# Expert pieces of eight blocks with stationary weights fetched from DRAM per block, on one Trainium2 core

## The chip, the core and the metric

The kernel runs on one core of a Trainium2 chip. The metric is device time in microseconds (us), from start to end of one execution. Within the core TensorE (PE) multiplies matrices, VectorE (DVE), ScalarE (ACT) and GpSimd (POOL) do elementwise work, and SyncE (SP) issues nearly all transfers (DMAs) from one queue, in the order of its program.

## The reference, cut to what matters

Two transformer layers work on x of shape (32, 256, 128). Each has attention with 16 heads of 8 features and then a feed-forward part of 16 experts, of which every token takes two. For the change only the experts matter:

```python
# layer 0 (weights per expert e: gate_up 128x128, down 64x128, with biases)
gate, up = minimum(gate, 7), clip(up, -7, 7)
act = (up + 1) * gate * sigmoid(1.702 * gate)
out = sum over the two chosen e of score_e * (act @ down_e + down_bias_e)
# layer 1 (no biases), plus a shared expert that the change leaves alone
act = silu(x @ Wg_e) * (x @ Wu_e)
out = sum over the two chosen e of w_e * (act @ Wd_e)
```

## The kernel before

**Units and steps.** A unit is one batch entry of one layer: 64 units, 16 heads each. The program of every engine is one loop over `step`; unit u computes the scores of head j at step 16u + j. In every step PE computes two products of scores, of one unit for the maxima (`ps_s`, line 1224) and of the unit before for the exponentials (`ps_st`, line 1230); DVE takes the maximum (line 1639), ACT the exponential (line 871). All engines go through the steps in pairs, here called rounds: a unit has eight. In a round PE issues the scores of both steps first and then `jobs(step)` and `jobs(step + 1)`: projections, transposes, probabilities times values (line 1093), and the experts' pieces. PE takes its instructions in order, so what one job waits for holds up all later ones, the scores too.

**Experts.** Units are taken in nine groups (`SIZES`, 8 units in the first six; groups 0 to 3 are layer 0). The tokens of a group are sorted by expert into blocks of 128 rows in DRAM (`slot_dram`, written by POOL, line 672), 48 blocks for a group of 8 units; a row of integers, `column`, says which expert a block belongs to. Blocks are worked on in pieces of `QB` = 4 (class `Quad`), 100 in all. A piece is loaded (SP, line 535), transposed on PE (line 1044), multiplied by gate and up weights that lie in SBUF for all 16 experts (lines 1061 and 1062), put through tanh and products (ACT, DVE, POOL), transposed back (line 1074), multiplied by the down weights (line 1081), taken by ACT (line 854) and stored (SP, line 545). Between, ACT also copies the two transposes (lines 828 and 847). PE loads the four experts' numbers into registers (line 1051), which are the column offsets into the weights. The outputs stand with tokens in rows.

**What sets the order.** The table `QUAD` gives the step at which each piece is transposed, `STAGE` the distance from it of each later stage; a piece's stages thus fall in fixed rounds. SP's order is the same for its queue. Per unit it issues, at fixed steps: six transfers of the projections to DRAM (`part_rows`, lines 502 and 505, at step 15 of the 16), four of 192 KB that bring them back as stacks (`stack_rows`, line 517, at step 4), the maxima out (`max_store`, line 482, at 7 and 15) and back (`max_rows`, line 492, at 10 and 2), and `mod_in` (line 582, at 12). Two of these wait for other engines at a place that matters below:

```python
def stack_rows(u):                       # SP, step 16u - 12
    ...
    if u.has(3):
        sp.wait_ge(st_mm, u.count(16, -32))
def max_rows(u, half):
    sp.wait_ge(mx_stored[half], u.count(16, 16))
```

The first holds SP at its step 4 until PE has issued the scores of its step 9, because the stacks have three buffers. The second waits until the maxima have landed in DRAM.

Of the kernel before, what the change touches and what calls it, by code (L numbers as in the profile page):

```python
# [41 lines left out]
QB = 4  # L42
# [9 lines left out]
LANES = 3  # L52
# [31 lines left out]
class Quad:  # L84

    def __init__(self, no):
# [11 lines left out]
        self.before_bank = first - 2 + min(self.lane, 1) if start else no - LANES if self.tail else no - 2  # L98
        self.blk = self.bank = self.lane if self.tail else self.par
# [20 lines left out]
for g in range(NG):  # L120
# [18 lines left out]
STAGE = {"blocks": (0, 0), "gate_up": (3, 3), "clip": (3, 3), "tanh": (5, 3), "act": (6, 3), "product": (7, 7), "act_t": (10, 6),  # L139
         "down": (15, 9), "store": (16, 10), "load": (-12, -5)}  # L140


def quad_at(step, stage):

    for quick, after in enumerate(STAGE[stage]):
        q = Quad(QUAD[step - after]) if step - after in QUAD else None
        if q and q.quick == quick:
            return q
# [18 lines left out]
def build(nc, io, out):  # L167
    with ExitStack() as ctx:
# [29 lines left out]
        wgu = [sb(f"wgu{l}", [P, E * 2 * F]) for l in range(2)]  # L198
        wd = [sb(f"wd{l}", [P, E * D]) for l in range(2)]
# [16 lines left out]
        b_stack = sb("b_stack", [P, 2 * E * F], BF16)  # L216
# [53 lines left out]

        g_sb = sb("g_sb", [P, QB, F])
        u_sb = sb("u_sb", [P, QB, F])
# [16 lines left out]
        stack = [q[:].rearrange("p h t -> p (h t)").bitcast(F32) for q in q_stk]  # L289
        h_blk = [sb("h_blk0", [P, QB * D])[:], sb("h_blk1", [P, QB * D])[:], stack[1][:, 0:QB * D]]  # L290
        h_blk_t = [sb("h_blk_t", [P, QB * P])[:], late[:, 0:512], late[:, 2048:2560]]
        act = [sb("act", [P, QB * P])[:], late[:, 512:1024], late[:, 2560:3072]]
        act_t = [sb("act_t", [P, QB * P])[:], late[:, 1024:1536], late[:, 3072:3584]]
        th_sb = [sb("th_sb", [P, QB * F])[:], late[:, 1536:1792], late[:, 3584:3840]]
        y_sb = [sb("y_sb", [P, QB * D])[:], stack[0][:, 0:512], stack[0][:, 512:1024]]
        ps_lane = [ps_q[0], ps_q[1], ps_s[0]]
# [12 lines left out]
        b_in = early[0:E, 29 * D:30 * D].rearrange("e (g f) -> e g f", g=2)  # L309
        b_rest = early[0:E, 30 * D:32 * D].rearrange("e (i c) -> e i c", i=2)  # L310
        b_part = sb("b_part", [E, 3, 2 * F], BF16)
# [5 lines left out]
        bias_dram = dram("bias_dram", (E, 3, 2 * F), BF16)  # L317
# [12 lines left out]
        bias_ok, bias_stored, bias_back = sem("bias_ok"), sem("bias_stored"), sem("bias_back")  # L330
# [4 lines left out]
        lanes_clear = sem("lanes_clear")  # L335
# [28 lines left out]
        tail_loaded = [sem(f"tail_loaded{i}") for i in range(LANES)]  # L364
        blk_mm, blk_t_ok = sem("blk_mm"), sem("blk_t_ok")
        gu_mm, clip_ok, th_ok, glu_ok, act_ok = (sem(n) for n in ("gu_mm", "clip_ok", "th_ok", "glu_ok", "act_ok"))
        act0_ok = sem("act0_ok")
        at_mm, at_ok, down_mm, y_ok = (sem(n) for n in ("at_mm", "at_ok", "down_mm", "y_ok"))
# [12 lines left out]
        REST_LOADS = 20  # L381
# [47 lines left out]
        def _(sp):  # L429
# [8 lines left out]
            sp.dma_start(b_in, io["b_gu"]).then_inc(rest_loaded, 16)  # L438
# [3 lines left out]
            for dst, name in ((wq[1], "wq1"), (wk[1], "wk1"), (wv[1], "wv1"), (wo[1], "wo1"), (wsgu, "wsgu"), (wsd, "wsd"),  # L442
                              (wgu[0], "wgu0"), (wd[0], "wd0"), (wgu[1], "wgu1"), (wd[1], "wd1")):
                sp.dma_start(dst[:], io[name]).then_inc(rest_loaded, 16)
# [81 lines left out]
            def quad_load(q):  # L526
# [4 lines left out]
                if q.no >= 2:  # L531
                    sp.wait_ge(blk_mm, q.before_bank + 1)
# [1237 lines left out]
```

## Time and profile before

| | before |
|---|---|
| median of 3 runs | 1712.38 us (1711.74 to 1713.73) |
| profiled execution, its own time | 1713.12 us |
| its span | 1711.4 us |
| granted TensorE clock, mean | 0.95 of full speed |
| PE, DVE, ACT, POOL busy | 83%, 79%, 68%, 59% |
| DMA packets | 392007, 234.70 MB |

Busy time is the union of an engine's instructions; a matmul's recorded length holds its way through the array, so the distance from one start to the next says more than the length. Rows with the engine "SPq" are transfers issued by SP's queue, with the time that the issue takes.

### The profile page before, as it was taken

The numbers are of one execution on the slowest core, as the hardware profiler recorded it, in microseconds if no ns is written. First come the engines' busy times: TensorE is split into PE (matmuls) and PEld (weight loads), VectorE is DVE, ScalarE is ACT, GpSimd is POOL, SyncE is SP. The second block draws the span as 40 slices with busy tenths as digits, with TensorE's granted clock in tenths as the row PEclk, the third lists the DMA queues.
The fourth block names the chain that finished last, engine by engine and source line by source line (L and its number), as shares of the span: only waits on it lengthen the run. The fifth ranks groups of instructions, "written<-read, shape, count | busy, mean of one in ns | idle before, by whom it ended". The sixth has DMA issues, their size and how long they took to land.

```text
span 1711.4 us, 44855 instructions
## 1 busy us (share of the span) xinstructions
PE 1424.6 (83%) x13909; PEld 915.6 (54%) x13909; DVE 1349.4 (79%) x4032; ACT 1171.5 (68%) x2708; POOL 1003.4 (59%) x1376
## 2 busy tenths in 40 slices
PE   2788888899899889988999989998999879885752
PEld 1244444456555556655666656655666646655641
DVE  5679989888888898898898998888888857643522
ACT  1487777678778777787777777787778757663432
POOL 1223225733584878576866778576765783487573
PEclk9999999899999999999999999999899989997866
DMA  6765556445555655566555556566556654444542
GB/s 202 172 154 148 134 137 154 120 119 126 134 150 141 141 136 140 145 141 134 131 147 137 124 128 156 132 144 131 130 149 136 155 135 116 110 117 124 150 132 73
DMA packets 392007, 234.70 MB, mean 137 GB/s; under 512 B 29007, under 2 KB 380561, under 8 KB 391267
## 3 DMA queue, kind: packets, MB, share of 16 engines
q1 hardware_dynamic: 356675, 188.82, 46.0%
q0 software_dynamic: 16384, 33.59, 7.3%
q10 hardware_dynamic: 18720, 9.44, 2.0%
q8 instruction: 121, 1.98, 0.5%
q14 instruction: 107, 0.88, 0.2%
HBM read 123.49 MB, written 108.17 MB: 135 GB/s over the span
## 4 chain that ended last, share of the span: by engine, by line
PE 38%; DVE 27%; POOL 17%; issue 11%; DMA 3%; ACT 2%; SPq 1%; POOLq 0%; DVEq 0%; ACTq 0%
DVE mx L1639 12%; PE ps_job L1093 7%; POOL slot_dram L672 6%; PE ps_s L1224 5%; PE ps_q L1062 4%; POOL y_in L693 3%; PE ps_q L1081 2%; PE ps_st L1230 2%; PE ps_job L1114 2%; PE ps_q L1044 2%; PE ps_q L1074 2%; PE ps_job L1197 1%; PE ps_job L1189 1%; PE ps_job L1144 1%; DVE h_mid L1414 1%
## 5 line engine op out<-in xcount | busy, mean ns | idle before, releaser
L1639 DVE TENSOR_REDUCE mx<-ps_s 128x2 f32<-128x512 f32 x1024 | 655.1, 682 | 98.8 <-PE ps_s L1224 97.5
L871 ACT ACTIVATE prob<-ps_st 128x512 f32<-128x512 f32 x1024 | 560.8, 596 | 80.5 <-PE ps_st L1230 78.3
L1224 PE MATMUL ps_s<-k_stk,q_stk 51*128 51x256 bf16 x2048 | 359.6, 280 | 102.2 <-DVE mx L1639 75.6
L1230 PE MATMUL ps_st<-q_stk,k_stk 53*128 53x256 bf16 x2048 | 352.5, 278 | 4.5 <-ACT prob L871 4.3
L1093 PE MATMUL ps_job<-prob,v_ext 128*32 128x256 f32 x4096 | 284.2, 396 | 22.7 <-issue 12.4
L672 POOL DMA_INDIRECT slot_dram<-h_row,slot x256 | 255.7, 999 | 71.2 <-issue 65.3
L1224 PEld LDWEIGHTS ps_s<-k_stk,q_stk 51*128 51x128 bf16 x2048 | 138.7, 95 | 286.5 <-DVE mx L1639 194.4
L693 POOL DMA_INDIRECT y_in<-y_dram,slot x224 | 222.4, 993 | 85.8 <-issue 50.1
L1093 PEld LDWEIGHTS ps_job<-prob,v_ext 128*32 128x32 f32 x4096 | 114.3, 111 | 127.6 <-issue 31.8
L807 ACT ACTIVATE o_sb<-ps_job 128x256 f32<-128x256 f32 x256 | 97.2, 380 | 110.2 <-PE ps_job L1093 100.5
L716 POOL TENSOR_TENSOR qk_rest<-qk_f,qk_part 128x512 f32<-128x512 f32 x64 | 74.4, 1163 | 138.6 <-ACT qk_part L905 138.1
L636 POOL TENSOR_SCALAR ln_ve<-ln_mv 128x2 f32<-128x2 f32 x128 | 28.7, 224 | 201.4 <-DVE ln_mv L1407 196.7
L1230 PEld LDWEIGHTS ps_st<-q_stk,k_stk 53*128 53x128 bf16 x2048 | 135.5, 95 | 14.9 <-ACT prob L871 5.9
L1062 PE MATMUL ps_q<-wgu,h_blk_t 128*128 x704 | 118.2, 301 | 0.0
L1062 PEld LDWEIGHTS ps_q<-wgu,h_blk_t 128*128 128x128 f32 x704 | 100.3, 198 | 9.4 <-issue 7.7
L1081 PE MATMUL ps_q<-wd,act_t 128*128 x704 | 99.7, 285 | 1.7 <-ACT act_t L847 1.7
L720 POOL TENSOR_TENSOR qk_part<-qk_rest,qk_part 128x512 bf16<-128x512 f32 x64 | 74.3, 1160 | 43.5 <-ACT qk_part L909 42.8
L638 POOL TENSOR_TENSOR ln_rs<-ln_ve,neg_half 128x2 f32<-128x2 f32 x128 | 92.0, 718 | 10.7
L1081 PEld LDWEIGHTS ps_q<-wd,act_t 128*128 128x128 f32 x704 | 86.6, 194 | 17.3 <-issue 17.3
L1044 PE MATMUL ps_q<-ident,h_blk 128*128 128x128 f32 x376 | 63.7, 295 | 35.3 <-DMA h_blk<-slot_dram 30.0
L1101 PE MATMUL ps_job<-ident,o_sb 128*128 128x128 f32 x512 | 79.4, 278 | 2.0 <-DVE sh_act L1597 2.0
L711 POOL TENSOR_TENSOR act<-th_sb,u_sb 128x256 f32<-128x256 f32 x48 | 35.3, 735 | 68.9 <-DVE th_sb L1581 68.8
(211 smaller groups left out, 2913.5 us busy)
## 6 DMA issues: line engine op xcount, KB each, us to landing
part_dram<-qk_part SPq DMA_DIRECT2D x128, 192.0 KB
q_stk<-part_dram SPq DMA_DIRECT2D x128, 192.0 KB
k_stk<-part_dram SPq DMA_DIRECT2D x128, 192.0 KB
h_blk<-slot_dram SPq DMA_DIRECT2D x94, 256.0 KB, 3.9
y_dram<-y_sb SPq DMA_DIRECT2D x88, 256.0 KB, 2.4
part_dram<-qk_part SPq DMA_DIRECT2D x128, 128.0 KB
mod_in<-row_dram SPq DMA_DIRECT2D x64, 192.0 KB
slot_dram<-sh_out ACTq DMA_DIRECT2D x18, 512.0 KB, 4.3
```

The lines of the kernel that those rows point to most:

```text
L638: pool.tensor_tensor(ln_rs[i][:], ln_ve[i][:], neg_half[:], ALU.pow).then_inc(ln_rstd[i], 1)
L672: pool.indirect_dma_start(slot_dram[u.group % 3], bass.IndirectOffsetOnAxis(ap=slot[u.group][:, i:i + 1], axis=0), h2_row[u.no % len(h2_ro ...
L693: pool.indirect_dma_start(y_rows[y_buf(u)[0]][:, j // 2, j % 2, :], None, y_dram[u.group % 3], bass.IndirectOffsetOnAxis(ap=slot[u.group][ ...
L807: sc.activation(o_sb[u.par][:, g, :], ps_job[BANK[f"av{g}"]][:, 0:S], ACT.Copy).then_inc(o_ok, 1)
L871: sc.activation(prob[:, (k ^ 1) % 8, :], ps_st[k % 2][:], ACT.Exp).then_inc(exp_done, 1)
L1044: mm = pe.transpose(ps_lane[q.bank][:, j * P:(j + 1) * P], h_blk[q.blk][:, j * D:(j + 1) * D], ident[:])
L1062: mm = pe.matmul(b[:, j * P:(j + 1) * P], h_blk_t[q.lane][:, j * P:(j + 1) * P], wgu[q.layer][:, w], start=q.layer == 1, stop=True)
L1081: mm = pe.matmul(ps_lane[q.bank][:, j * P:(j + 1) * P], act_t[q.lane][:, j * P:(j + 1) * P], wd[q.layer][:, bass.ds(expert[q.bank][j], P)] ...
L1093: mm = pe.matmul(columns(f"av{g}")[32 * i:32 * i + 32, 0:S], v_ext[u.par][:, kt, h, :], prob[:, h % 8, kt * S:(kt + 1) * S], start=kt == 0 ...
L1224: mm = pe.matmul(ps_s[j % 2][:, t * S:(t + 1) * S], q_stk[us.tri][r0:r0 + R_BIAS, hp, t * P:(t + 1) * P], k_stk[us.tri][r0:r0 + R_BIAS, hp ...
L1230: mm = pe.matmul(ps_st[k % 2][:, t * S:(t + 1) * S], k_stk[ut.tri][r1:r1 + R_MAX, hp, t * P:(t + 1) * P], q_stk[ut.tri][r1:r1 + R_MAX, hp, ...
L1639: dve.tensor_reduce(mx[:, hp // 4, :, 4 * par + hp % 4], ps_s[j % 2][:].rearrange("p (t s) -> p t s", s=S), AX_X, ALU.max).then_inc(max_do ...
```

## The change

`QB` becomes 8 (50 pieces). The weights of all experts are no longer in SBUF. For each block SP reads the expert's number into a register and issues a transfer of that expert's 128x256 weights (gate, up, down, 128 KB) from DRAM to one of two buffers `w_q` (three in the tail), and in layer 0 a second one of three bias rows. These are spread over eight steps, from 8 before the piece's transpose to 1 before it. PE waits for all eight before it begins with the gate. The weights are the stationary operand, so gate and up come out with features in rows: blocks are taken in pairs, the even one in partitions 0 to 63, the odd one in 64 to 127, gate in one PSUM bank and up in another. The activations then already lie as the down product needs them, so that the transpose back and ACT's copy of it go; the down product reads 64 rows of an even block and 64 of an odd one, into two banks. The pieces of the first five groups are transposed at steps 6, 12 and 0 of their units (three in four units, the fourth unit has only later stages), those of group 5 at step 6 of each unit. Tail lanes become 2 instead of 3.

```diff
-QB = 4
+QB = 8
+PAIRS = QB // 2
+EW = 2 * F + D
...
-        QUAD[last + 147 + 32 * (i // 3) + (0, 11, 21)[i % 3] if late < 0 else
-             END + (-109 + 8 * i, -11 + 6 * i, 56 + 4 * i, 112 + 4 * i)[late]] = PIECE_AT[g] + i
+        QUAD[last + 150 + 64 * (i // 3) + (0, 22, 42)[i % 3] if late < 0 else
+             END + (-106 + 16 * i, -8 + 12 * i, 56 + 8 * i, 112 + 8 * i)[late]] = PIECE_AT[g] + i
...
-STAGE = {"blocks": (0, 0), "gate_up": (3, 3), "clip": (3, 3), "tanh": (5, 3), "act": (6, 3), "product": (7, 7), "act_t": (10, 6),
-         "down": (15, 9), "store": (16, 10), "load": (-12, -5)}
+STAGE = {"load": (-12, -12, -5), "weights": (-8, -8, -6), "blocks": (0, 0, 0), "gate": (4, 4, 3), "up": (6, 6, 3), "clip": (6, 0, 0),
+         "clip_up": (8, 0, 0), "tanh": (8, 6, 4), "act": (10, 8, 6), "product": (11, 0, 0), "down": (14, 12, 8), "y": (16, 14, 10),
+         "store": (18, 16, 11)}
...
-        wgu = [sb(f"wgu{l}", [P, E * 2 * F]) for l in range(2)]
-        wd = [sb(f"wd{l}", [P, E * D]) for l in range(2)]
+        w_q = [sb(f"w_q{i}", [P, QB, EW]) for i in range(2)]
+        b_q = [sb(f"b_q{i}", [P, QB, EW], BF16) for i in range(2)]
...
+            def quad_weights(q, j):
+
+                if j == 0:
+                    sp.wait_ge(column_ok, q.group + 1)
+                    if q.before_buf is None:
+                        sp.wait_ge(av_mm, 4 * UNITS)
+                    elif q.before_buf >= 0:
+                        sp.wait_ge(down_mm, q.before_buf + 1)
+                b = q.i * QB + j
+                sp.reg_load([regs[j]], column[q.group % 3][0:1, b:b + 1])
+                first = bass.ds(sp.snap(regs[j], min_val=0, max_val=(E - 1) * EW), EW)
+                sp.dma_start(w_q[q.buf][:, j, :], io[f"we{q.layer}"][:, first]).then_inc(w_loaded[q.buf], 16)
+                if q.layer == 0:
+                    sp.dma_start(b_q[q.buf][F * (j % 2):F * (j % 2) + 3, j, :], bias_dram[:, first]).then_inc(b_loaded[q.buf], 16)
...
+                for j in range(QB):
+                    q = quad_at(step - j, "weights")
+                    if q:
+                        quad_weights(q, j)
...
+            def quad_gate_up(q, part):
+
+                pe.wait_ge(w_loaded[q.buf], q.uses * QB * 16)
+                pe.wait_ge(blk_t_ok, 2 * q.no + 2)
+                if q.layer == 0:
+                    pe.wait_ge(b_loaded[q.buf], q.uses * QB * 16)
+                f = slice(part * F, (part + 1) * F)
+                for p in range(PAIRS):
+                    outs = [ps_lane[q.lane][part][F * h:F * h + F, p * P:(p + 1) * P] for h in range(2)]
                     if q.layer == 0:
-                        pe.matmul(b[:, j * P:(j + 1) * P], ones_b[:], b_stack[:, w], start=True, stop=False)
-                    mm = pe.matmul(b[:, j * P:(j + 1) * P], h_blk_t[q.lane][:, j * P:(j + 1) * P], wgu[q.layer][:, w],
-                                   start=q.layer == 1, stop=True)
+                        for h in range(2):
+                            pe.matmul(outs[h], b_q[q.buf][:, 2 * p + h, f], ones_b[:], start=True, stop=False, skip_group_check=True)
+                    for h in range(2):
+                        j = 2 * p + h
+                        mm = pe.matmul(outs[h], w_q[q.buf][:, j, f], h_blk_t[q.lane][:, j * P:(j + 1) * P],
+                                       start=q.layer == 1, stop=True, skip_group_check=True)
                 mm.then_inc(gu_mm, 1)
...
+                for p in range(PAIRS):
+                    for h in range(2):
+                        rows = slice(F * h, F * h + F)
+                        mm = pe.matmul(ps_lane[q.lane][h][:, p * P:(p + 1) * P], act[q.lane][rows, p * P:(p + 1) * P],
+                                       w_q[q.buf][rows, 2 * p + h, 2 * F:EW], start=q.layer == 1, stop=True, skip_group_check=True)
                 mm.then_inc(down_mm, 1)
```

On SP, at step 4 of a unit whose piece is transposed at step 6 (layer 0), the stacks come back (line 517 before, 521 now). Before, the queue held there:

```order
L517 DMA q_stk<-part_dram 48x8x256 x2
L517 DMA k_stk<-part_dram 48x8x256 x2
L482 DMA max_dram<-mx_t 16x256
L535 DMA h_blk<-slot_dram 128x4x128
L492 DMA q_stk<-max_dram 2x1024 x2
```

Now the weights of the last two blocks stand behind the stacks, each with its register load, `w_q` the weights and `b_q` the bias rows; the second block's rows repeat the first's:

```order
L521 DMA q_stk<-part_dram 48x8x256 x2
L521 DMA k_stk<-part_dram 48x8x256 x2
L552 TENSOR_LOAD column
L553 ISA
L554 DMA w_q<-in_we 128x256
L556 REGISTER_ALU
L556 DMA b_q<-bias_dram 3x256
L552 TENSOR_LOAD column
```

So two of the eight transfers that this piece's gate waits for are issued only after SP's wait at the stacks. For a piece that is transposed at step 12 it is all eight (steps 4 to 11).

Also on SP, in layer 0, the last block of a piece that is transposed at step 0 comes behind the projections' way out and a store of maxima, at step 15:

```order
L506 DMA part_dram<-qk_part 128x3x256
L506 DMA part_dram<-qk_part 128x2x256
L506 DMA part_dram<-qk_part 128x256
L509 DMA part_dram<-qk_part 128x3x256
L509 DMA part_dram<-qk_part 128x2x256
L509 DMA part_dram<-qk_part 128x256
L486 DMA max_dram<-mx_t 16x256
L552 TENSOR_LOAD column
L553 ISA
L554 DMA w_q<-in_we 128x256
```

Before, nothing of the experts stood between that store and the next `max_rows`.

On PE, gate and up of a piece in layer 0 stood behind one wait before, for ACT's copy of the transpose (1093 are the values of the round):

```order
L1093 MATMUL ps_job<-prob,v_ext 32x256 [waits exp_done,v_ok,mxt_ok]
L1093 MATMUL ps_job<-prob,v_ext 32x256 x7
L1061 ISA [waits blk_t_ok]
L1061 MATMUL ps_q<-b_stack,ones_b 128x128
L1062 ISA
L1062 MATMUL ps_q<-wgu,h_blk_t 128x128
```

The gate now begins with three waits (1238 are the scores of the round):

```order
L1238 MATMUL ps_st<-q_stk,k_stk 128x256
L1072 MATMUL ps_q<-ones_b,b_q 64x128 [waits b_loaded0,blk_t_ok,w_loaded0]
L1072 MATMUL ps_q<-ones_b,b_q 64x128
L1075 MATMUL ps_q<-h_blk_t,w_q 64x128 x2
L1072 MATMUL ps_q<-ones_b,b_q 64x128 x2
```

Four such pairs make the gate. Its waits stand ahead of the round's remaining jobs and of all scores that follow.

## Rows read from the trace of the kernel before

**Rows 1.** The page: busy time by engine.
```profile
PE 1424.6 (83%) x13909; PEld 915.6 (54%) x13909; DVE 1349.4 (79%) x4032; ACT 1171.5 (68%) x2708; POOL 1003.4 (59%) x1376
```
**Rows 2.** Stretches of one unit: length, then busy us (instructions) of PE, PEld, DVE, ACT, POOL.
```profile
149.80:168.40 18.60, 15.30 (x171) 8.04 (x172) 17.03 (x51) 14.42 (x34) 5.71 (x11) 1.00 0.66 155
...
385.80:406.60 20.80, 19.21 (x205) 11.99 (x205) 18.84 (x58) 17.47 (x41) 7.96 (x15) 1.00 0.52 117
406.60:428.30 21.70, 20.29 (x218) 13.47 (x217) 17.32 (x52) 16.68 (x40) 5.72 (x11) 1.00 0.56 134
889.30:911.30 22.00, 21.68 (x221) 14.14 (x221) 20.14 (x64) 17.84 (x42) 8.52 (x16) 1.00 0.51 114
```
**Rows 3.** Rounds of steps 6 and 8 in the first of those units; columns as before.
```profile
157.00:158.60 1.60, 1.34 (x20) 0.86 (x21) 1.57 (x6) 1.58 (x4) 0.76 (x2) 1.00 0.02 5
158.60:161.60 3.00, 2.86 (x30) 1.43 (x29) 2.04 (x7) 2.07 (x7) 0.59 (x3) 1.00 0.35 94
```
**Rows 4.** Timeline of PE: start, us, engine, line, operation, tiles, count; jobs of pieces.
```profile
599.99 0.22 PE L1061 MATMUL ps_q<-b_stack,ones_b 128*128 x1
...
600.32 0.22 PE L1061 MATMUL ps_q<-b_stack,ones_b 128*128 x1
...
601.63 1.07 PE L1093 MATMUL ps_job<-prob,v_ext 128*32 128x256 f32 x16
602.63 1.16 PE L1081 MATMUL ps_q<-wd,act_t 128*128 x8
...
610.20 0.66 PE L1074 MATMUL ps_q<-ident,act 128*128 128x128 f32 x4
```
**Rows 5.** Timeline of SP's queue over one unit, from the stacks on.
```profile
397.58 0.83 SPq L517 DMA_DIRECT2D q_stk<-part_dram  x2
398.45 0.99 SPq L517 DMA_DIRECT2D k_stk<-part_dram  x2
399.54 0.41 SPq L482 DMA_DIRECT2D max_dram<-mx_t  x1
...
405.26 0.54 SPq L492 DMA_DIRECT2D q_stk<-max_dram  x2
...
406.32 0.45 SPq L582 DMA_DIRECT2D mod_in<-row_dram  x1
406.87 1.46 SPq L502 DMA_DIRECT2D part_dram<-qk_part  x3
408.38 1.62 SPq L505 DMA_DIRECT2D part_dram<-qk_part  x3
```
**Rows 6.** Waits of SP's queue over the span: line, releaser, us, times, longest.
```profile
SPq L492 <- DMA max_dram<-mx_t: 344.8, 123, 5.4
SPq L513 <- PE ps_st L1230: 285.1, 59, 7.7
```
**Rows 7.** Timeline of PE over the same unit: last scores, jobs of steps 8, 10, 16, 20.
```profile
397.20 0.27 PE L1230 MATMUL ps_st<-q_stk,k_stk 53*128 53x256 bf16 x1
...
397.40 1.07 PE L1093 MATMUL ps_job<-prob,v_ext 128*32 128x256 f32 x16
...
400.01 0.23 PE L1143 MATMUL ps_job<-bo_stack,ones_b 128*128 128x128 bf16 x1
...
407.32 1.07 PE L1093 MATMUL ps_job<-prob,v_ext 128*32 128x256 f32 x16
...
412.88 1.07 PE L1093 MATMUL ps_job<-prob,v_ext 128*32 128x256 f32 x16
```
**Rows 8.** Instructions of line 1051: durations in ns, min/median/max.
```profile
L1051 PEldq TENSOR_LOAD <-column x100: 327/333/1091, 347.6 to 1672.4; - x100
```
**Rows 9.** Page, transfers: KB each, median us from issue to landing.
```profile
y_dram<-y_sb SPq DMA_DIRECT2D x88, 256.0 KB, 2.4
```
**Rows 10.** A stretch with PE mostly idle, and the next; PEclk third from the end.
```profile
1373.30:1378.00 4.70, 0.79 (x8) 0.29 (x8) 0.34 (x2) 2.26 (x7) 4.08 (x5) 1.00 0.38 111
1378.00:1381.40 3.40, 3.35 (x20) 1.86 (x20) 3.29 (x13) 2.33 (x6) 3.01 (x4) 0.50 0.16 43
```

More of the change, by code:

```diff
@@ L51 @@
 RING = 4
-LANES = 3
+LANES = 2
 PLAN = 9
@@ L878, in rest @@
                         take_o(u, g)
-                q = quad_at(step, "blocks")
-                if q:
-                    take_blocks(q)
+                for half in range(2):
+                    q = quad_at(step - half, "blocks")
+                    if q:
+                        take_blocks(q, half)
                 q = quad_at(step, "tanh")
@@ L884, in rest @@
                     tanh_gate(q)
-                q = quad_at(step, "act_t")
-                if q:
-                    take_act(q)
-                q = quad_at(step, "down")
-                if q:
-                    take_y(q)
+                for half in range(2):
+                    q = quad_at(step - half, "y")
+                    if q:
+                        take_y(q, half)
                 u = at(step, -33)
@@ L1028, in columns @@
                 return ps_job[BANK[name]][:, COLUMN[name]:]
-            regs = [[ctx.enter_context(pe.register(f"expert{lane}_{j}")) for j in range(QB)] for lane in range(LANES)]
-            expert = [None] * LANES
             def quad_transpose(q):
@@ L1064, in quad_gate_up, with quad_down @@
                 mm.then_inc(gu_mm, 1)
-            def quad_act(q):
+            def quad_down(q):
                 pe.wait_ge(*act_done(q))
-                if q.tail and q.lane and q.nth == 0:
-                    pe.wait_ge(lanes_clear, q.lane)
                 if q.layer == 0:
-                    pe.wait_ge(clip_ok, 2 * q.no + 2)
-                for j in range(QB):
-                    mm = pe.transpose(ps_lane[q.bank][:, j * P:(j + 1) * P], act[q.lane][:, j * P:(j + 1) * P], ident[:])
-                mm.then_inc(at_mm, 1)
@@ L1077, in quad_down @@
-            def quad_down(q):
-                pe.wait_ge(at_ok, q.no + 1)
-                for j in range(QB):
-                    mm = pe.matmul(ps_lane[q.bank][:, j * P:(j + 1) * P], act_t[q.lane][:, j * P:(j + 1) * P],
-                                   wd[q.layer][:, bass.ds(expert[q.bank][j], P)], start=True, stop=True)
+                    for h in range(2):
+                        pe.matmul(ps_lane[q.lane][h][:], ones_b[F * h:F * h + F, :], b_q[q.buf][F * h:F * h + F, h::2, 2 * F:EW], start=True, stop=False,
+                                  skip_group_check=True)
@@ L1642, in rest @@
             def rest(step):
-                q = quad_at(step, "clip")
-                if q:
-                    quad_clip(q)
+                for part, stage in enumerate(("clip", "clip_up")):
+                    q = quad_at(step, stage)
+                    if q and q.layer == 0:
+                        quad_clip(q, part)
                 q = quad_at(step, "act")
```

206 lines of the change are left out of this document (88 added, 118 removed).

## The prediction

> **What bounds the kernel now.** I read the page's busy line first: PE 83% and DVE 79% [rows 1], so neither alone, and asked for stretches of one unit. A unit without experts takes 18.6 us and DVE is busy for 17.03 of them; with experts it takes 20.8 and 21.7 us in layer 0 (two units hold three old pieces) and 22.0 in layer 1, and there PE fills nearly all: 21.68 of 22.0 [rows 2]. Single rounds say why. The round of steps 6 and 7 has DVE busy for 1.57 of 1.60 us, while that of 8 and 9 has PE busy for 2.86 of 3.00 and DVE for 2.04 [rows 3]. Since scores have two banks, neither engine can run far ahead, and a round takes about as long as the busier of the two in that round. Work taken from PE is therefore worth its time only in rounds where PE is the longer. The 12 blocks of two layer-0 units lengthen these units by 20.8 + 21.7 - 2 x 18.6 = 5.3 us, or 0.44 us a block.
>
> Then SP, since the change adds to its queue. It has no busy time on the page, but waits: 344.8 us for the maxima to land in DRAM, and 285.1 us in 59 waits at the stacks, for PE [rows 6]. So SP has slack on average, but it isn't free to use it when it likes: at every unit it stands at step 4 until PE is in the round of steps 8 and 9. The timelines show it: the stacks go out at 397.58, just after that round's jobs begin on PE at 397.40 [rows 5, 7].
>
> **What goes from PE.** The price of a job is the distance between starts. In layer 0 a block's gate and up take 600.32 - 599.99 = 0.33 us; the eight instructions of a down product about 1.0, so 0.22 a block; a transpose of four about 0.5, or 0.13 a block [rows 4]. The transpose back goes: -0.13 a block. The down product now works with 64 rows at a time, even and odd blocks in different halves of the array and in different banks; the values' product already puts four narrow products beside each other (sixteen instructions of 256 columns in 1.0 us, while eight of 128 columns at full width take about as long [rows 4], so per column four times as fast or near it). I take half: -0.11 a block, and +0.03 for its bias in layer 0. Gate and up are twice as many instructions, each half as wide, two beside each other: unchanged. Sum: -0.21 a block in layer 0, -0.24 in layer 1, for 400 blocks -90 us of PE's work. Laid over the rounds by the tables `QUAD` and `STAGE`, with 1.0 us for eight transposes, 1.3 for a gate or an up (0.9 in layer 1) and 1.1 for a down, each round as long as the busier engine, the 24 blocks of four layer-0 units lengthen them by 7.8 us, 0.33 a block; the same count for the old table gives 4.9 us for 12, 0.41 (the trace: 0.44). In layer 1 it gives 4 us less for 24 blocks. So 0.085 x 192 + 0.17 x 96 = 32 us, and about 10 for the 112 late blocks, by halves of these rates: **-42 us**. ACT loses 100 copies and DVE and POOL take fewer, longer instructions; they are not the longer engine in the rounds where the gate stands, and DVE's part is in the count. Both ends: 0 if PE's saving falls in rounds that DVE holds, -90 if every round is PE's.
>
> A rule speaks against the halves. The skill ("TensorEngine Tiling (Array Packing)", Key Properties, in the Trainium skill) says that a change of the tiling mode drains TensorE; each down would add one or two. In this trace the values at 397.40 start 0.2 us after the last scores at 397.20, which need about half of that themselves [rows 7]; so a change costs 0.1 us at most, and the sum leaves it out. With 0.1 us at each of some 150 changes it would be 15 us more.
>
> **What comes to SP, and when it is due.** A block costs SP a register load, 0.33 us on PE [rows 8], a transfer to 128 partitions, 0.45 us as `mod_in`, in layer 0 one of three rows, 0.27 us as each of the two of line 492 [rows 5], and 0.1 for the gaps and register arithmetic: 1.2 us in layer 0, 0.9 in layer 1. The average would fit: 6 blocks a unit are 7 us, against about 10 us a unit of waiting (344.8 + 285.1 over 64). But the places don't. From the release at the stacks in the shown unit:
>
> - Transpose at step 6. Stacks are out at 399.5. The seventh block's issue ends at 400.7, the eighth's transfer is issued at 401.1. The gate is due at step 10, whose jobs begin at 400.01 [rows 7]. A transfer takes 2.4 us to land at the median of the stores [rows 9], so 403.5 at the earliest; but behind the four stacks even the small store of maxima, issued at 399.54, had landed only by 405.26 [rows 5]. I take 405: PE stands for **5 us** (3.5 to 6). The same in layer 1.
> - Transpose at step 12, all eight behind the stacks: 399.5, three blocks 3.6, store 0.4, one block 1.2, a store of y 0.4, two blocks 2.4, the maxima's two 0.6, one block 1.2 and the last register load: issued at 409.8, landed at 412.2. Due at step 16, 407.32 [rows 7]: **5 us**; in layer 1 blocks are 0.3 us cheaper and the rounds a little longer: 2.
> - Transpose at step 0 of the next unit, blocks at steps 8 to 15: two blocks and two transfers to 402.8, the maxima landed at 406.3 or so, then 0.6, three blocks 3.6, `mod_in` 0.5, a block, a store, a block (2.8), the six of `part_rows` 3.2 [rows 5], a store 0.4, the last block's register load: issued at 417.9, landed at 420.6, behind the projections. Due at step 20, 412.88 [rows 7], plus 1 us of the piece before: **6.7 us**; in layer 1 about 4.
>
> Groups 0 to 3 have 8 such sets of three (16.7 us each), group 4 two (11 us), group 5 six of the first kind (5 us), and the first piece of group 6 is of this kind too: 134 + 22 + 30 + 5 = **+191 us**. While PE stands at the gate everything behind it stands: the rest of the jobs, the next scores, and with them the maxima and exponentials. No engine has work in store for more than a round.
>
> The DMA page of the Trainium skill ("DMA: Bandwidth & Descriptors", Latency and other measured facts) gives about 600 ns as the floor of a register load. The trace has 333 ns on PE [rows 8], and I go by that. By the page the second kind would be about 2 us later and the third too, some 35 us more in all, an estimate from that page.
>
> **The clock.** In the 4.70 us from 1373.30 PE is busy for 0.79; the 3.4 us behind it ran at 0.50 granted, 1.2 instead of 2.4 GHz [rows 10]. Most of the new stops are longer. 3.4 us at half the clock put off 1.7 us of PE's work; DVE hides some of it, so +1 us each for some 32: **+32 us**. Both ends: 0, and 60 where a stop costs two such stretches.
>
> **Head and tail.** 4 MB of weights fewer are loaded at the start, which nothing waits for at its end; one more clearing of a bias buffer on DVE adds about a microsecond. The tail is led by POOL's transfers, and SP needs 8 us a piece there (eight times 0.9 and two transfers), about what two old pieces took. I put both at 0 (-5 to +15).
>
> **Sum** against the profiled execution's own time, which is 0.7 us above the median: 1713 + 191 + 32 - 42 = 1894; I say 1890.
>
> **Rivals.**
> 1. *The weights arrive in time*, and only PE's saving stays: 1713 - 42 = **1671 us**, faster. For it: SP's slack on average, and that the loads begin 8 steps (about 11 us) ahead. Against: the order of the queue. It would need the last block to land within 2.4 us of SP's release at the stacks, which the 405.26 row speaks against. It decides for faster as soon as a piece waits less than 42/50 = 0.8 us on average. 0.15.
> 2. *The half-wide products don't run beside each other.* Then gate and up take twice as long, +1.8 us for eight blocks, 90 us, of which half is exposed by the rate found above: +45, and with the stops **1935 us**. For it: only four columns and bf16 rows are shown running side by side, never two halves in f32. Against: the same unit does it with four. 0.10.
> 3. *The stops are there but half as long*, because transfers overtake the stacks' backlog: 3.5, 2 and 4 us in layer 0, 3.5, 0 and 2 in layer 1, 21 and 3 for the late groups: 76 + 11 + 24 = 111, clock 15: **1797 us**. 0.20.
> 4. The forecast itself, 1890: 0.53. The remaining 0.02 is that gains and stops cancel.
>
> The range goes down to rival 3 with PE's saving at its bound of 90 and nothing for the clock, 1797 - 48 - 15 = 1734, and up to rival 2 with the clock at its bound and 12 us for the tail, 1935 + 28 + 12 = 1975. The measurement of this kernel can tell about 0.2% from no change. Faster than that 0.15, within it 0.02, slower 0.83.
>
> **What would show each step.** Idle time of PE ahead of the first instruction of a gate (line 1072 in layer 0, 1075 in layer 1), released by DMA `w_q`, some 32 times for 3 to 7 us; none in rounds without a gate. SP's waits at the stacks (285.1) fall by well over 100 us. More stretches at 0.50. Lines of gate, up and down: starts 0.11 us apart for two halves. ACT busy lower by its 100 copies, PE busy lower by some 90 us. The forecast is wrong if the weights' landings show no wait at the gates, or if SP's register loads are so cheap or the queue so short that the second and third kinds vanish; the first kind is what I am surest of.

## The result, and the profile after

The changed kernel takes 2034.4 us at the median of 4 runs (2032.0 to 2038.9), the kernel before beside it 1713.1: a ratio of 1.188 (95% interval 1.185 to 1.191). The forecast was 1890, with a range that ended at 1975. The direction and the stops that were to cause it were right; the size of +177 was little more than half of the measured +321, and PE's saving of 42 us, which it counted, did not come.

The page of the changed kernel, which answers to [rows 1]:

```profile
PE 1436.9 (71%) x14549; PEld 887.6 (44%) x14549; DVE 1337.8 (66%) x3906; ACT 1095.7 (54%) x2558; POOL 1000.6 (49%) x1352
...
PEclk9999998878887887887788888888898879798866
```

PE is busy for 12 us more than before and DVE, ACT and POOL for less, but the span has 319 us more. PE's granted clock is 0.86 on average where it was 0.95, and mostly 0.8 from the seventh slice on. (PE has less work in its 1436.9 us than in the 1424.6 of before: 562 us of this span ran at 0.50, where it was 170.) The waits, PE's first and then those of SP's queue, say where the idle time lies:

```profile
PE ps_q L1072 <- DMA w_q<-in_we: 96.9, 13, 9.9
...
PE ps_q L1072 <- DMA b_q<-bias_dram: 83.3, 11, 9.7
PE ps_q L1075 <- DMA w_q<-in_we: 76.3, 19, 7.7
```
```profile
SPq L517 <- PE ps_st L1238: 286.7, 51, 10.0
SPq L496 <- DMA max_dram<-mx_t: 242.7, 97, 5.3
```

43 stops at the gates (lines 1072 and 1075), 257 us, most of what the change costs. SP's wait at the stacks is 286.7 us, and was 285.1 before [rows 6]: the blocks took their time from SP, and the stops that they made gave it back there. Four units in a row, columns as in [rows 2], show that units with a gate are long and the one without (the second) is not:

```profile
463.70:494.60 30.90, 21.79 (x231) 13.94 (x232) 20.22 (x63) 15.46 (x37) 6.97 (x11) 0.78 0.51 130
494.60:515.70 21.10, 17.67 (x198) 10.06 (x198) 18.07 (x55) 16.16 (x39) 16.52 (x22) 1.00 0.61 157
515.70:546.20 30.50, 20.80 (x237) 12.71 (x239) 18.27 (x52) 15.61 (x37) 17.95 (x23) 0.83 0.59 144
546.20:580.20 34.00, 21.37 (x243) 13.45 (x243) 18.94 (x54) 16.39 (x39) 17.50 (x25) 0.80 0.46 118
```

One stop of the second kind, first on SP's queue and then on PE. SP is released at the stacks at 506.03; a block comes every 1.56 us; the last issue ends at 522.3:

```profile
506.03 0.84 SPq L521 DMA_DIRECT2D q_stk<-part_dram  x2
506.91 0.99 SPq L521 DMA_DIRECT2D k_stk<-part_dram  x2
508.69 0.37 SPq L554 DMA_DIRECT2D w_q<-in_we  x1
509.25 0.31 SPq L556 DMA_DIRECT2D b_q<-bias_dram  x1
510.25 0.36 SPq L554 DMA_DIRECT2D w_q<-in_we  x1
...
521.49 0.36 SPq L554 DMA_DIRECT2D w_q<-in_we  x1
522.03 0.28 SPq L556 DMA_DIRECT2D b_q<-bias_dram  x1
```
```profile
516.30 0.27 PE L1238 MATMUL ps_st<-q_stk,k_stk 53*128 53x256 bf16 x1
524.11 0.32 PE L1072 MATMUL ps_q<-ones_b,b_q 128*64 128x128 bf16 x2 [7.54 <-DMA b_q<-bias_dram]
...
524.62 0.34 PE L1072 MATMUL ps_q<-ones_b,b_q 128*64 128x128 bf16 x2
...
526.38 0.66 PE L1101 MATMUL ps_job<-prob,v_ext 128*32 128x256 f32 x4
```

PE has issued its scores and stands 7.54 us for the bias rows of the eighth block, which SP issued 2.1 us before. The gate then takes 526.38 - 524.11 = 2.27 us at a granted clock of 0.50; at 1.00 it takes 1.23 (below).

### The profile page after: what moved, and what is told of

It is laid out like the page before. It is cut to its first block, busy times and chain, and to the rows that moved or that the text cites. A ratio compares the mean times of both kernels' runs of the same rounds, so it can differ in the third digit from the quotient of the medians.

```text
span 2030.3 us, 46535 instructions
## 1 busy us (share of the span) xinstructions
PE 1436.9 (71%) x14549; PEld 887.6 (44%) x14549; DVE 1337.8 (66%) x3906; ACT 1095.7 (54%) x2558; POOL 1000.6 (49%) x1352
## 2 busy tenths in 40 slices
DMA packets 448578, 283.37 MB, mean 140 GB/s; under 512 B 34269, under 2 KB 437631, under 8 KB 448337
## 4 chain that ended last, share of the span: by engine, by line
PE 25%; SPq 19%; DVE 15%; POOL 14%; issue 13%; DMA 11%; ACT 2%; POOLq 0%; DVEq 0%; ACTq 0%
DVE mx L1638 7%; PE ps_job L1101 5%; POOL slot_dram L695 5%; PE ps_q L1075 5%; SPq L552 4%; SPq L554 3%; DMA w_q<-in_we 3%; PE ps_s L1232 3%; SPq L521 3%; DMA max_dram<-mx_t 3%; POOL y_in L716 3%; SPq L556 3%; DMA h_blk<-slot_dram 1%; SPq L509 1%; SPq L506 1%
## 5 line engine op out<-in xcount | busy, mean ns | idle before, releaser
L1232 PE MATMUL ps_s<-k_stk,q_stk 51*128 51x256 bf16 x2048 | 368.6, 284 | 127.7 <-DVE mx L1638 87.4
L1238 PE MATMUL ps_st<-q_stk,k_stk 53*128 53x256 bf16 x2048 | 362.3, 282 | 0.4
L1101 PE MATMUL ps_job<-prob,v_ext 128*32 128x256 f32 x4096 | 304.6, 419 | 26.3 <-issue 11.1
L1075 PE MATMUL ps_q<-h_blk_t,w_q 128*64 128x128 f32 x1408 | 151.7, 366 | 81.7 <-DMA w_q<-in_we 76.3
L1072 PE MATMUL ps_q<-ones_b,b_q 128*64 128x128 bf16 x384 | 55.2, 277 | 180.2 <-DMA w_q<-in_we 96.9
L1075 PEld LDWEIGHTS ps_q<-h_blk_t,w_q 128*64 128x64 f32 x1408 | 108.9, 192 | 91.9 <-DMA w_q<-in_we 81.4
L1238 PEld LDWEIGHTS ps_st<-q_stk,k_stk 53*128 53x128 bf16 x2048 | 135.8, 96 | 12.2 <-issue 2.7
L1664 DVE TENSOR_TENSOR att_tmp<-ps_job,mod_in 128x256 f32<-128x256 f32 x64 | 27.0, 422 | 143.9 <-PE ps_job L1166 142.9
L1072 PEld LDWEIGHTS ps_q<-ones_b,b_q 128*64 128x64 bf16 x384 | 29.6, 142 | 193.3 <-DMA w_q<-in_we 186.5
L876 ACT ACTIVATE sh_th<-ps_job 128x256 f32<-128x256 f32 x64 | 24.9, 389 | 141.0 <-PE ps_job L1197 140.3
L728 POOL TENSOR_TENSOR x<-x,att_tmp 128x256 f32<-128x256 f32 x64 | 47.2, 737 | 103.9 <-DVE att_tmp L1664 103.5
```

What stands on the lines that cost most here:

```text
L1072: pe.matmul(outs[h], b_q[q.buf][:, 2 * p + h, f], ones_b[:], start=True, stop=False, skip_group_check=True)
L1075: mm = pe.matmul(outs[h], w_q[q.buf][:, j, f], h_blk_t[q.lane][:, j * P:(j + 1) * P], start=q.layer == 1, stop=True, skip_group_check=True)
L1101: mm = pe.matmul(columns(f"av{g}")[32 * i:32 * i + 32, 0:S], v_ext[u.par][:, kt, h, :], prob[:, h % 8, kt * S:(kt + 1) * S], start=kt == 0 ...
L1232: mm = pe.matmul(ps_s[j % 2][:, t * S:(t + 1) * S], q_stk[us.tri][r0:r0 + R_BIAS, hp, t * P:(t + 1) * P], k_stk[us.tri][r0:r0 + R_BIAS, hp ...
L1238: mm = pe.matmul(ps_st[k % 2][:, t * S:(t + 1) * S], k_stk[ut.tri][r1:r1 + R_MAX, hp, t * P:(t + 1) * P], q_stk[ut.tri][r1:r1 + R_MAX, hp, ...
```

## Experiments

"Early" below means that the weights are issued 20 steps ahead, "resident" that they lie in SBUF. Each row of this table is a run that is told below. Times are medians, ratios are to the kernel before, run beside it on the same chip: e6 to e8, e9 to e12 and e13 to e16 come from three chips, on which the kernel before took 1714.3, 1713.6 and 1714.3 us. The kernels with constant addresses or constant experts (e2, e3, e7, e9, e10, e11, e14, e16) leave out the choice of the expert by the data.

| run | edit | us | ratio (95%) |
|---|---|---|---|
| e6 | the changed kernel again | 2036.9 | 1.188 (1.183 to 1.192) |
| e8 | early weights | 1779.1 | 1.039 (1.036 to 1.042) |
| e13 | early, one register load a piece | 1732.6 | 1.010 (1.008 to 1.012) |
| e14 | early, one transfer a piece | 1707.5 | 0.996 (0.995 to 0.998) |
| e7 | resident, bias over 64 rows | 1753.8 | 1.022 (1.015 to 1.029) |
| e9 | resident, PE exactly as changed | 1713.9 | 1.000 (0.998 to 1.002) |
| e16 | e9 with gaps filled | 1708.2 | 0.996 (0.995 to 0.997) |
| e10 | changed, constant addresses | 1942.6 | 1.134 (1.131 to 1.138) |
| e15 | changed, one register load a piece | 1967.8 | 1.148 (1.146 to 1.150) |
| e11 | changed, one transfer a piece | 1967.8 | 1.149 (1.145 to 1.153) |
| e12 | changed, stops filled with products | 2006.5 | 1.172 (1.167 to 1.176) |

The runs e1 to e4 came first, on a fourth chip, on which the kernel before itself took 1809 us (1803 to 1819) and every time was longer; their ratios are told beside the repeats, e5 to e8, e10 and e12, which are taken as the measurement. (An expectation below says that loads of 512 KB landed late on that chip. The traces do not show it: such loads, of `w_res`, landed in 6.0 us at the median there and in 5.9 us on the chip of e7.)

**Weights earlier.** Does the place in SP's queue make the stops?

```diff
-    q = quad_at(step - j, "weights")        # 8 steps ahead (6 in groups 6 to 8)
+    q = weights_at(step - j)                # 20 ahead in groups 0 to 5, 14 in group 6, 6 in 7 and 8
```

> The weights of a piece are issued over the eight steps that begin 20 steps before its transpose instead of 8 (14 instead of 8 or 6 for the pieces of group 5; groups 6 to 8 as before). All of them then stand in SP's queue ahead of the stacks of step 4 that they stood behind. Theory A, the place in the queue: the stops at the gates vanish outside the last three groups, and what stays is the changed kernel less about 43 stops: 1713 - 42 for PE's saving + 12 for the tail + 2 for the head = about 1685 us. Theory B, SP's time: a block costs SP about 1.55 us in layer 0, six a unit are 9.3, and SP had 9.8 us of waiting a unit before the change, most of it waiting that it can't shift. Then the lateness only moves, to the stacks or the maxima, and the time stays above 1850 us.

1872.3 us there, ratio 1.036 (1.031 to 1.041). (By the kernel's tables it is group 6, not group 5, whose pieces get 14 steps.) Four kernels were run again on another chip, with the kernel before among them for its trace:

> The kernel before, unchanged, for a trace of it from the same chip as the runs beside it: in the call with the early and the resident weights it took 1809 us instead of 1713. If the chip is the cause, this run goes with its neighbours and the comparison of stages holds within the call.

1711.0 us (one run): this chip is like that of the first result.

> The changed kernel, unchanged, beside the others: ratio to the kernel before 1.19 if the chip doesn't matter; on a chip where the kernel before takes 1809 us, 1.13 if this chip's slowness is hidden in the stops at the gates (2040 us, as the kernel with constant addresses there).

2036.9 us, 1.188.

> The weights 20 steps ahead again. It had no stop at a gate outside the tail, so it should stand within 10 us above the resident kernel on any chip; if SP's time is short, it stands over 20 us above it.

1779.1 us. No gate of groups 0 to 5 waits any more, and 258 us are gone: theory A as to the stops, though not its 1685 us. For 65 us stay against the kernel before, and theory B has a part in them. Some lateness has moved to the maxima. Timeline of SP's queue in the early kernel, and PE at the same place:

```profile
541.50 0.29 SPq L564 DMA_DIRECT2D b_q<-bias_dram  x1
542.48 0.35 SPq L562 DMA_DIRECT2D w_q<-in_we  x1
543.00 0.29 SPq L564 DMA_DIRECT2D b_q<-bias_dram  x1
543.35 0.54 SPq L504 DMA_DIRECT2D q_stk<-max_dram  x2
```
```profile
545.03 0.37 PE L1240 MATMUL ps_s<-k_stk,q_stk 51*128 51x256 bf16 x1 [5.91 <-issue]
```

The rows of maxima (line 504, due at step 2) stand behind six blocks of weights, and PE's scores wait for them 5.91 us; "issue" says only that the profile found no releaser. They start 1.7 us after the issue of that transfer. Over the span PE's scores wait for transfers or without a releaser for 41 us in this kernel, and for 6 in e9 below.

**Fewer issues at the early place.** One register load for eight numbers; then one transfer of the same 1 MB for all eight blocks (constant address, biases of the first two pieces for all).

```diff
                 if j == 0:
...
-                b = q.i * QB + j
-                sp.reg_load([regs[j]], column[q.group % 3][0:1, b:b + 1])
+                    sp.reg_load(regs, column[q.group % 3][0:1, q.i * QB:(q.i + 1) * QB])
```

> Early weights, and one register load for the eight numbers of a piece instead of eight. The early kernel lost 57 us against the kernel with weights in SBUF between units 16 and 44, where pieces are of layer 0, and nothing in layer 1. If that is SP's issue time, seven loads of 0.46 us fewer a piece, or 2.4 us a unit, bring back most of it: 1730 to 1750 us against 1779. If it is the traffic of 49 MB, the time stays at 1779.

1732.6 us, as forecast. The load of eight numbers in e13 takes 712 ns at the median, that of one in the changed kernel 457 (view of one line's instructions: min/median/max in ns), so a piece saves about 3 us on SP:

```profile
L552 SPq TENSOR_LOAD <-column x400: 260/457/1092, 345.0 to 1992.5; - x134
```
```profile
L559 SPq TENSOR_LOAD <-column x50: 522/712/1272, 331.1 to 1679.7; - x50
```

> The single transfer of 1 MB a piece at a constant address, issued with the early places (the eighth of the eight steps that begin 20 before the transpose; output not the reference's). Bytes as in the changed kernel, but a sixteenth of the issues. SP's issue time as the cause: within 10 us of the kernel with weights in SBUF, 1714 to 1725 us. Traffic as the cause: 1770 or more.

1707.5 us. The traffic (283 MB against 235), moved in large pieces, costs nothing that can be seen, and nothing of the 65 us is left. 46 of them are the seven register loads a piece (e13, with the same transfers). Another 25 went with the small transfers as a whole, bias rows and address arithmetic included: e14 has fewer issues and also fewer and larger packets (397106 against 448578), and no run tells the two apart. (The expectations call the units up to 44 those of layer 0; pieces of layer 0 in fact run to unit 47. The loss between 44 and 47 was below 1 us.)

**Weights in SBUF.** What is PE's new arrangement worth alone? 16 KB of each partition hold one layer's weights for all experts; layer 1's are loaded once, between the layers.

```diff
-    w_q = [sb(f"w_q{i}", [P, QB, EW]) for i in range(2)]
+    w_res = sb("w_res", [P, E * EW])
...
-    mm = pe.matmul(outs[h], w_q[q.buf][:, j, f], h_blk_t[q.lane][:, j * P:(j + 1) * P],
+    mm = pe.matmul(outs[h], of_expert(w_res, slice(0, P), q, j, part * F, F), h_blk_t[q.lane][:, j * P:(j + 1) * P],
...
```

> No weight transfers: the layer's weights and biases lie in SBUF for all experts (loaded at the start, and the second layer's once between the layers), everything else on PE, ACT, DVE and POOL as in the changed kernel. The expert of a block is a constant of the program (block number modulo 16) and not the one of the row of integers, so the output is not the reference's. My term for PE's saving says 1713 - 42 = 1671 us (0 to -90: 1713 to 1623). The rival, that half-wide products don't run beside each other or that DVE holds the rounds anyway, says 1713 or more.

1860.0 us there, 1.029 (1.024 to 1.033).

> The kernel with a layer's weights in SBUF again (constant experts, output not the reference's). If its ratio of 1.0285 belongs to the new arrangement of pieces (my term of -42 us was wrong in sign), it shows 1.02 to 1.03 on any chip; if it belongs to that chip, where loads of 512 KB landed late, it falls below 1.00 here.

1753.8 us, 1.022: not the chip. The timeline of a gate shows what part was mine. First e7, with bias products of 64 rows by 64 columns between products of 128 by 64, then the early kernel with both at 128 by 64:

```profile
398.44 0.24 PE L1075 MATMUL ps_q<-ones_b,b_res 64*64 64x128 bf16 x2
398.61 0.44 PE L1079 MATMUL ps_q<-h_blk_t,w_res 128*64 128x128 f32 x4
398.98 0.24 PE L1075 MATMUL ps_q<-ones_b,b_res 64*64 64x128 bf16 x2
```
```profile
557.35 0.25 PE L1080 MATMUL ps_q<-ones_b,b_q 128*64 128x128 bf16 x2
557.43 0.39 PE L1083 MATMUL ps_q<-h_blk_t,w_q 128*64 128x128 f32 x4
557.65 0.22 PE L1080 MATMUL ps_q<-ones_b,b_q 128*64 128x128 bf16 x2
...
558.58 0.23 PE L1159 MATMUL ps_job<-bo_stack,ones_b 128*128 128x128 bf16 x1
```

A pair of blocks takes 0.54 us in e7 and 0.28 to 0.30 here: the two changes of the tile's shape cost some 0.25 us, 0.12 each, and a gate 2.17 instead of 1.23. The Trainium skill ("TensorEngine Tiling (Array Packing)", Key Properties) says that a change of the tiling mode drains the engine; these rows agree that it costs time.

> As the resident kernel, but with PE's instructions exactly those of the changed kernel: the bias rows of gate and up are read over all 128 rows again. In the first resident kernel they were read over 64 rows only, and a gate or up of eight blocks took 2.17 us there in layer 0 against 1.23 in the kernel with early weights; that is 24 x 2 x 0.94 = 45 us of PE's work that was mine and not the change's. Experts are constants of the program, the output is not the reference's. If my term for PE's saving (-42, bounds 0 and -90) is right, the time falls from 1.022 to 0.98 of before (about 1675 us; with half of the 45 exposed, 1730 at most). If the pieces of eight in single rounds cost as much as PE saves, it stays at 1.00 to 1.02.

1713.9 us, the time before (0.998 to 1.002). So e7's 40 us are those changes of shape (24 x 2 x 0.94 = 45 us of work; e7's down products also add their bias in other pieces, 1.27 us each for 1.20, under 2 us in all). The new arrangement, without its fetching, gains nothing. Yet it does less work, as the stretch from unit 16 to 44 shows in e5 (before), in e9, and in e16 below (columns as in [rows 2]; one execution each, and e9's, 1718.6 us, is the longest of its ten):

```profile
345.20:985.20 640.00, 580.13 (x6005) 373.79 (x6007) 562.63 (x1660) 497.48 (x1149) 411.39 (x572) 0.98 0.57 137
```
```profile
345.60:989.90 644.30, 554.52 (x6393) 342.12 (x6393) 557.72 (x1602) 462.27 (x1085) 408.83 (x553) 0.96 0.56 136
```
```profile
348.20:980.30 632.10, 553.02 (x6451) 341.07 (x6453) 557.45 (x1602) 462.78 (x1084) 408.44 (x552) 0.98 0.58 139
```

PE has 25.6 us less to do and DVE 4.9, and the stretch is 4.3 us longer. Two rounds of unit 17 in e9, steps 2 and 4, show how time is lost:

```profile
368.50:372.25 3.75, 1.37 (x14) 0.65 (x16) 3.72 (x10) 1.54 (x4) 1.26 (x1) 0.97 0.54 146
372.25:377.10 4.85, 4.85 (x48) 3.19 (x50) 3.32 (x11) 1.58 (x3) 1.16 (x3) 0.67 0.30 87
```

In the first DVE is busy for 3.72 of 3.75 us, where e5's same round has 1.97 of 2.07. Its own rows say with what:

```profile
368.85 0.68 DVE L1586 SCALAR_TENSOR_TENSOR th_sb<-th_sb,g_sb 128x512 f32<-128x512 f32 x1
...
369.60 1.26 POOL L722 TENSOR_TENSOR act<-th_sb,u_sb 128x512 f32<-128x512 f32 x1 [1.24 <-DVE th_sb L1586]
...
369.64 1.25 DVE L1446 TENSOR_TENSOR mx_part<-mx,mx_part 128x16 bf16<-128x16 f32 x1
```

The activation of eight blocks, now in one piece, takes 0.68 us. More goes to a small instruction (L1446) that takes 0.175 us at the median and 1.25 here, beside POOL's product of the same piece; what holds it, the trace does not say. Before, POOL's products were half as long (0.73 us), and the longest of the same instruction was 0.64 us (e5).

PE works 1.37 us in this round and waits. In the next one it has the down product of the same piece, and runs it at 0.50. The crowded round is not even needed for that: among the eight such units of layer 0 it is long in four (3.8 to 4.3 us; 2.0 to 2.8 in the others), but PE has only 1.2 to 1.4 us of work in it each time, and the next round has a mean clock of 0.53 to 0.70 in all eight. So work that was even is now in lumps; and PE, with less to do, falls to the lower clock 13 times in this stretch where it fell 5 times (54 us at 0.50 against 20).

**Filling gaps.** Idle moments of PE filled with products that nobody uses.

```diff
+    if q and q.layer == 0 and q.i % 3 == 0:          # behind the jobs of the step of the activation
+        pe.wait_ge(clip_ok, 2 * q.no + 2)
+        for _ in range(8): pe.matmul(ps_lane[0][0][:], ones_b[:], <ident_b four times>, start=True, stop=True)
```

> The kernel with weights in SBUF and PE's own program, and eight products of 512 columns in bf16 (1.7 us at full clock, unused) behind the jobs of the round with DVE's activation of each first piece of layer 0, where PE then waited 2.3 to 3.1 us for the maxima and ran the next round, with the down product, at 0.50. If the clock ate PE's saving, seven or eight stretches at 0.50 go and each gives back 1.5 us: -11 us, 1703 against 1714. If the half clock is hidden behind DVE there, no change or a few us more.

1708.2 us: 6 less than e9 over the whole (the intervals of the two ratios, 0.995 to 0.997 and 0.998 to 1.002, do not touch, but the kernels ran on two chips). In the stretch above it is 12.2 less in the two profiled executions (632.1 against 644.3), 7.2 of it in steps 0 to 5 of the seven units with the filling, with 7 falls to 0.50 instead of 13. More work for PE and a shorter time: so part of the vanished saving was the clock. The rest (640.0 - 632.1 = 8 us are gained of 26 saved) I put down to the lumps; no run shows that part by itself.

The same in the changed kernel, 16 such products ahead of each gate of groups 0 to 5:

> Ahead of the wait for the weights at each gate of groups 0 to 5 PE runs 16 products of 512 columns in bf16 (about 3.4 us at full clock) into the bank that the gate then overwrites; what they compute isn't used. They fit in the stop where it is longer than that. If the clock's fall behind the stops costs what the count of stretches at 0.50 says (68 against 24 of some 3.4 us at half the clock, up to 75 us), the time falls by 30 to 60 us, to about 1985 us, with fewer such stretches. If the lower clock is hidden behind DVE, the time stays or rises by the few stops that are shorter than the filling.

2090.6 us there (one run; the kernel before 1809), a ratio of 1.156, on a chip on which the changed kernel itself was not run.

> The filling of the stops with products again, beside its neighbours. If the lower clock behind the stops costs 30 to 60 us, about 1985 us against 2035. If the time is no lower than 2035 although the clock is higher, the clock is not a term that adds to the stops.

2006.5 us against e6's 2036.9: -30 (by the ratios, as the chips differ, 27), and 362 us at 0.50 instead of 595. That is the lower end of what was expected.

**What the stops are made of.** Three edits at the late place:

```diff
-    sp.reg_load([regs[j]], column[q.group % 3][0:1, b:b + 1])
-    first = bass.ds(sp.snap(regs[j], min_val=0, max_val=(E - 1) * EW), EW)
+    first = slice(b % E * EW, b % E * EW + EW)                # e3, e10
```

> Every weight and bias transfer of the changed kernel stays where it is, but at a constant address (block number modulo 16), without the register load and its arithmetic, so the output is not the reference's. If the stops are SP's issue time behind the stacks, each block behind the stacks saves some 0.5 to 0.6 us: two blocks in the first kind (-1 us), seven or eight in the other two (-4 us each), for 8 sets about -70 us and some 10 in the late groups, about 1950 us. If the landing of 1 MB a piece sets the stops, the time stays at 2034 us.

2042.9 us there (one run), a ratio of 1.129.

> The constant addresses again (no register load on SP, output not the reference's), on the chip of its neighbours. On the other chip it took 2043 us where before took 1809. If a block behind the stacks costs SP 0.5 us less, about 1950 to 1970 us here against 2035; if only the landing counts, 2035.

1942.6 us, -94.

> The changed kernel with one register load for the eight numbers of a piece and nothing else changed. The constant addresses took 1943 us (-93). The register arithmetic stays, so a little less: 1945 to 1965 us. If the loads were not what the constant addresses saved, 2035.

1967.8 us, -69: the loads were most of it. The 25 us to e10 are the arithmetic and the longer load.

> Instead of eight register loads, eight weight transfers and eight bias transfers a piece: one transfer of the same 1 MB of weights (eight neighbouring experts, a constant address) at the step of the eighth, and the biases of the first two pieces for all; output not the reference's. Same bytes, a sixteenth of the issues, but issued at the latest place. If SP's issues set the stops: kind 1 keeps a landing behind the stacks (some 4 to 5 us, since 1 MB lands in about the time that two 512 KB loads take, 5 us each), kinds 2 and 3 go down to 0 to 2: about 1713 - 42 + 8 x 6 + 40 = 1760 us. If the bytes set them, 1 MB issued at once is later than eight spread transfers and the time is at least 2035 us.

1967.8 us: my 1760 was far off. SP's queue in e11, one piece of the first kind:

```profile
460.61 0.99 SPq L521 DMA_DIRECT2D k_stk<-part_dram  x2
461.63 0.47 SPq L553 DMA_DIRECT2D w_q<-in_we  x1
```

PE's gate starts at 468.45, 6.8 us later: 1 MB behind 768 KB of stacks lands no sooner than that, however few issues it takes (the profile's page gives 6.8 us at the median). Idle time of PE ahead of a gate, in us, mean over the eight pieces of layer 0 of each kind, read from the timelines:

| kind (transpose at step) | forecast | changed | e15 | e10 | e11 |
|---|---|---|---|---|---|
| 1 (6) | 5 | 5.5 | 4.7 | 4.6 | 6.4 |
| 2 (12) | 5 | 7.8 | 4.4 | 2.9 | 2.5 |
| 3 (0) | 6.7 | 9.2 | 6.9 | 5.5 | 5.3 |

Kind 1, with two blocks behind the stacks, is for the most part (4.6 of 5.5 us) made by the landing. In kinds 2 and 3, with eight, SP's issue time makes what e10 takes away, 4.9 and 3.7 us; about the 2.5 and 5.3 us that one late transfer leaves stay.

## Why the prediction was right or wrong

Of the 144 us between 1890 and 2034, 53 are the stops (point 5), 42 PE's saving (point 2), 14 the clock (point 6, an estimate), 11 head and tail (point 7), 5 my rounding and the time before; some 20 are not found. Two steps failed: the laying of PE's saving over the rounds, and SP's cost of a block, from which the length of the stops was reckoned.

1. **The bound** (a round is as long as the busier of PE and DVE) held where no transfer was late; the two rounds of e9 show it at its plainest.
2. **What goes from PE, -42 us: wrong, 0 measured (e9).** The pieces were priced well: a gate of eight blocks 1.23 us in layer 0 for my 1.3 and 1.02 in layer 1 for 0.9; PE's busy time 1355 in e9 against 1422 in e5, 67 less for my 90; a gate and an up of eight blocks (2.46 us) cost no more in layer 0 than those of two old pieces (1.43 us each), so halves run beside each other and rival 2 falls. (One reading in the sum is off: eight instructions of 1.0 us for four blocks are 0.25 a block, not 0.22; the new down product takes 0.12 a block, and 0.15 in layer 0, as I took it.) The step that failed is laying them over the rounds: I wrote that DVE's longer instructions aren't in the rounds where the gate stands, and looked no further. What the runs show lies in other rounds: the activation and POOL's longer product fall into a round that DVE already filled, PE has 1.2 to 1.4 us of work there, and the clock is at 0.50 in the next. The count had neither that delay nor that clock. The bound "0 if PE's saving falls in rounds that DVE holds" was the right end.
3. **Changes of the tiling mode, at most 0.1 us each:** about 0.12 in e7. Leaving out 15 us for the down products alone is not contradicted.
4. **SP's cost of a block, 1.2 and 0.9 us: too small in layer 0.** 1.56 and 0.8 were measured. The register load takes 457 ns at the median on SP where PE's took 333 [rows 8], and register arithmetic comes once for the weights and once for the bias rows. The floor of 600 ns that the Trainium skill gives ("DMA: Bandwidth & Descriptors", Latency and other measured facts) is above the 457 ns that this trace shows; by it the sum would have come 35 us nearer.
5. **The stops, +191: right in kind, too short.** The 37 gates of the sum stand for the reason given, for 244 us together, and 6 more in groups 6 to 8 for 12: the 43 stops above. Kind 1 was near the forecast. Kinds 2 and 3 were short by 2.8 and 2.5 us: eight blocks at the 0.36 us of point 4 are 2.9, and taking 2.9 us of loads a piece off SP's queue (e15) made these two kinds 3.4 and 2.3 us shorter. So that one number explains most of it: the 8 sets, 5.8 us longer each, are 46 of the 53 us. The other 7 lie in group 4, where kinds 2 and 3 stood for 3.7 to 7.7 us (forecast 2 and 4).
6. **The clock, +32: the right order, not closed.** Filling the stops gave back 30 (e12) while it took away 233 of the 360 us at 0.50 by which the changed kernel exceeds e9 (595 against 235); by proportion 46 in all, an estimate. PE's busy time, 1437 against 1355 us in e9 for as many instructions, allows up to 82.
7. **Head and tail, 0:** head +1.7 us; the tail from unit 63 took 254.7 us, against 243.0 before and 245.7 in e9: +9 to +12.
8. **What would show it:** waits for `w_q` or the bias rows came at the 37 gates of the sum, for 1.9 to 9.9 us (forecast: some 32, of 3 to 7). That PE's busy time falls by some 90 us was wrong in the changed kernel, where it rose by 12 with the lower clock (68 falls to 0.50 where there were 25). That SP's stack waits fall by over 100 us was wrong (286.7 for 285.1), because, as I read it, each stop gives SP its slack back at the next stacks. ACT lost its 100 copies (1095.7 for 1171.5 us).

The sum by measured terms: 1714 + 0 (e9) + 244 (stops) + 46 (clock) + 11 (head and tail) = 2015; about 20 us stay unassigned. The terms of the clock and of PE's saving come from other kernels than the changed one, so the sum is a check and no proof. Rival 1's condition, weights in time, can be met by the table alone: e8 met it at 1779, e13 with one load a piece at 1733, and e14, without true addresses, at 1707. That none is far below the time before is point 2 and SP's time. Of the kernels with true addresses none is below the time before.

## What to carry to other kernels

An issue queue with slack on average is a schedule, not a budget: ask for each transfer what stands ahead of it at its due time, and put what can go early ahead of the waits; here twelve steps were worth 258 us and one number in a table. Price a register load on the queue that will do it, and load a piece's numbers at once. When work is taken from one of two engines that alternate as the bound, and the rest is made into larger pieces, look at the rounds in which the other engines get their larger pieces, and at the clock behind the rounds that are left thin: in e9 a saving of 67 us of PE's busy time came to nothing there.

## What the hardware showed that was not expected

- A register load costs by the instruction, hardly by the number: one number 457 ns, eight 712 ns on SP; four 333 ns on PE.
- 48 MB more of transfers, 20% of all, cost nothing measurable when issued early and in large pieces (e14 at 0.996).
- A DVE instruction on 128 by 16 elements took 1.25 us beside a product of 1.26 us on POOL, and 0.175 us at the median (e9).
- Products that nobody uses made two kernels faster, by 6 and 30 us, while the time at half the clock fell (from 235 to 223 us and from 595 to 362 us). Nothing else was changed but the wait that goes with them in e16.
- One chip of those used ran the same kernel before in 1809 us where the others took 1713; in e2 there and e7, the same kernel, the first 13 units end within 3 us of each other (287.3 and 290.3 us), and the spans are 1857.7 and 1755.4. Why stays open.
